# Products of key features and values moved beside the next key features in an attention and feed-forward kernel

## The reference

```python
q_prime = relu(einsum('bhnd,fd->bhnf', q, Wqf))
k_prime = relu(einsum('bhnd,fd->bhnf', k, Wkf)) * mask
kv = einsum('bhnf,bhne->bhfe', k_prime, v)
qkv = einsum('bhmf,bhfe->bhme', q_prime, kv)
qk_sum = einsum('bhmf,bhf->bhm', q_prime, k_prime.sum(2))
x = x + (qkv / (qk_sum + 1e-8)) @ Wo.T + bo
# feed-forward, on layernorm(x); rows rounded to 127 steps, weights to -1, 0, 1
activated = up * square(relu(gate))
activated = activated * rsqrt(mean(square(activated)) + 1e-6) * g
x = x + bit_linear(activated, w_down)
```

## Time and profile before

| | |
|---|---|
| median of 3 runs | 430.47 us (430.22 to 432.01) |
| profiled execution | 431.65 us, span 429.6 us |
| PE busy | 411.4 us (96%) |
| VectorE busy | 342.3 us (80%) |
| ScalarE busy | 286.5 us (67%) |
| GpSimd busy | 145.8 us (34%) |
| chain that ended last | PE 52%, DVE 21%, issue 7%, ACT 7%, POOL 6%, DMA 6% |
| DMA | 42.42 MB, mean 99 GB/s |

### The profile page before, as it was taken

How to read it: one execution, slowest core, us unless ns; L and a number is a source line. 1 busy time by engine, 2 the same in 40 slices (tenths; PEclk the granted TensorE clock), 3 DMA queues, 4 the chain that set the end, 5 groups by cost and what they waited for, 6 DMA issues and landing times.

```text
span 429.6 us, 11266 instructions
## 1 busy us (share of the span) xinstructions
PE 411.4 (96%) x4804; PEld 284.4 (66%) x4835; DVE 342.3 (80%) x505; ACT 286.5 (67%) x406; POOL 145.8 (34%) x290
## 2 busy tenths in 40 slices
PE   8989999999999999999989999999999999999995
PEld 4879899988878945844754575575567566464443
DVE  4644659658679959899986897999998798998982
ACT  5655989892155287778449747765873878939960
POOL 0000000003054722483371545547325523344660
PEclk9989999999999999999999999999999999999999
DMA  7992474632050300113323033031213021413065
GB/s 235 418 403 74 169 278 159 287 120 82 24 198 5 108 19 2 32 31 87 73 38 63 0 88 76 11 75 50 51 41 70 14 50 27 84 62 75 1 146 124
DMA packets 51170, 42.42 MB, mean 99 GB/s; under 512 B 43056, under 2 KB 44080, under 8 KB 49200
## 3 DMA queue, kind: packets, MB, share of 16 engines
q1 hardware_dynamic: 51120, 41.70, 32.9%
HBM read 27.01 MB, written 4.19 MB: 73 GB/s over the span
## 4 chain that ended last, share of the span: by engine, by line
PE 52%; DVE 21%; issue 7%; ACT 7%; POOL 6%; DMA 6%; SPq 0%; DVEq 0%; ACTq 0%
PE ps L538 11%; PE ps L407 11%; PE ps L358 6%; PE ps L360 5%; PE ps L359 5%; PE ps L555 4%; DVE zb L974 3%; PE ps L429 2%; PE ps L514 2%; DMA xqT<-xqb 2%; PE ps L448 2%; DVE rows_of L922 2%; DVE tk L985 2%; DVE qol L933 1%; DVE rows_of L917 1%
## 5 line engine op out<-in xcount | busy, mean ns | idle before, releaser
L538 PE MATMUL ps<-tg,xqT 128*128 128x512 bf16 x243 | 58.1, 380 | 4.6 <-DMA xqT<-xqb 2.9
L538 PE MATMUL ps<-tu,xqT 128*128 128x512 bf16 x245 | 59.1, 379 | 1.3 <-issue 0.6
L555 PE MATMUL ps<-td,yqT 128*128 128x512 bf16 x202 | 45.9, 379 | 1.1 <-DMA yqT<-yqb 0.7
L538 PEld LDWEIGHTS ps<-tg,xqT 128*128 128x128 bf16 x256 | 23.5, 98 | 33.1 <-DMA xqT<-xqb 4.0
L538 PEld LDWEIGHTS ps<-tu,xqT 128*128 128x128 bf16 x256 | 24.2, 98 | 31.2 <-issue 3.0
L721 ACT ACTIVATE rb<-zb 128x1024 f32<-128x1024 f32 x29 | 30.6, 1055 | 20.7 <-DVE zb L974 20.5
L974 DVE TENSOR_TENSOR zb<-ps,rb 128x1024 f32<-128x1024 f32 x29 | 35.3, 1218 | 8.2 <-ACT rb L717 8.0
L358 PE MATMUL ps<-aph,wqh 128*128 128x256 f32 x128 | 37.2, 290 | 0.0
L360 PE MATMUL ps<-aph,wkl 128*128 128x256 f32 x124 | 35.4, 286 | 1.8 <-issue 1.8
L985 DVE TENSOR_REDUCE tk<-zb 128x1 f32<-128x1024 f32 x30 | 36.2, 1207 | 1.0 <-POOL zb L1189 0.7
L358 PE MATMUL ps<-aph,wkh 128*128 128x256 f32 x124 | 36.2, 292 | 0.6 <-issue 0.6
(11 more groups left out here) (153 smaller groups left out, 1037.1 us busy)
## 6 DMA issues: line engine op xcount, KB each, us to landing
xs<-in_wg_dram SPq DMA_DIRECT2D x4, 1024.0 KB, 13.9
xs<-in_wu_dram SPq DMA_DIRECT2D x4, 1024.0 KB, 6.6
xs<-in_wd_dram SPq DMA_DIRECT2D x4, 1024.0 KB, 7.9
xs<-in_x_dram SPq DMA_DIRECT2D x8, 512.0 KB, 4.9
out_dram<-xs SPq DMA_DIRECT2D x15, 256.0 KB, 2.0
craw<-in_ctx_dram SPq DMA_DIRECT2D x7, 512.0 KB, 5.8
xs<-in_wk_dram SPq DMA_DIRECT2D x4, 256.0 KB, 5.0
xs<-in_wv_dram SPq DMA_DIRECT2D x4, 256.0 KB, 6.6
```

Source lines behind the costliest of these rows:

```text
L538: k = pe.matmul(ps[:, b0 + n, :], xqT[:, i % 3, kc, :], tern[w][:, o:o + 512], start=kc == 0, stop=kc == KC - 1)
L555: k = pe.matmul(ps[:, D_BANK[i], :], yqT(i)[:, j, :], tern[2][:, 512 * j:512 * j + 512], start=j == 0, stop=j == 15)
```

## The change

`KV_BANK` becomes 6 for every batch, so that `key_values` writes banks 6 and 7, those of `keys`. On PE the order in the key stage becomes `keys(b)`, `values(b)`, `key_values(b-1)`, `key_features(b)`. `key_values(b-1)` waits for `key_rows` 1 and 3 of batch b, and `keys(b+1)` for both copies of `key_values(b-1)`; `key_values(6)` waits for `xT_lo(1)`. `total(0)` and `total(2)` stand directly before `values`, `total(1)` between `values(3, 1)` and `key_values(2)`, which now waits for `w_mean(1)`. `U_BANK` names the banks of `up`, with the values that they had; the signals of the ternary steps are listed in the new order. From `transpose(0)` on PE's order is the same; some of its waits are other ones. The lists of ScalarE, VectorE, GpSimd and SyncE are reordered all through, most calls by one to three places. `x1_normed(0)` also waits for `key_values(7)`.

```diff
-KV_BANK = (0, 0, 0, 0, 0, 0, 0, 6)
+KV_BANK = (6, 6, 6, 6, 6, 6, 6, 6)
+U_BANK = (2, 2, 2, 2, 2, 2, 2, 2, 2, 2, 2, 2, 2, 2, 2, 2, 2, 2, 2, 2, 2, 2, 2, 2, 2, 2, 2, 6, 2, 6, 2, 6)
...
-            keys(1); values(1, 0, range(12), v_rows.at(0, 0)); key_values(0); values(1, 1, range(12))
-            key_features(1, (0, kvc_rows.at(0, 0)), (1, kvc_rows.at(0, 1))); keys(2); total(0); key_values(1)
-            values(2, 0, range(12), w_mean.at(0)); values(2, 1, range(12))
-            key_features(2, (0, kvc_rows.at(1, 0)), (1, kvc_rows.at(1, 1))); keys(3); key_values(2); values(3, 0, range(12))
-            values(3, 1, range(12)); total(1); key_features(3); keys(4, w_mean.at(1)); key_values(3)
...
+            keys(1); values(1, 0, range(12), v_rows.at(0, 0)); values(1, 1, range(12), v_rows.at(0, 1))
+            key_values(0, kT_rows.at(1, 1), kT_rows.at(1, 3)); key_features(1)
+            keys(2, kvc_rows.at(0, 0), kvc_rows.at(0, 1)); total(0); values(2, 0, range(12), w_mean.at(0))
+            values(2, 1, range(12)); key_values(1, kT_rows.at(2, 1), kT_rows.at(2, 3)); key_features(2)
+            keys(3, kvc_rows.at(1, 0), kvc_rows.at(1, 1)); values(3, 0, range(12), v_rows.at(2, 0))
+            values(3, 1, range(12), v_rows.at(2, 1)); total(1); key_values(2, w_mean.at(1)); key_features(3)
+            keys(4, kvc_rows.at(2, 0), kvc_rows.at(2, 1)); values(4, 0, range(12)); values(4, 1, range(12))
...
+            values(7, 0, range(4, 12)); key_values(6, xT_lo.at(1)); values(7, 1, range(6)); queries(0, 0, kvc_rows.at(6, 0))
...
@@ scalar, key stage @@
-            scaled_weights(0, 0); key_values_copy(1, 0); key_values_copy(1, 1)
-            for n in range(1, 4):
+            for n in range(3):
                 scaled_weights(0, n)
-            context_hi(4, 0); magnitudes(1, 0); key_rows(3, 0); magnitudes(1, 1); key_rows(3, 1); key_rows(3, 2)
-            magnitudes(1, 2); key_values_copy(2, 0); key_values_copy(2, 1); key_rows(3, 3); magnitudes(1, 3)
+            key_values_copy(1, 0); scaled_weights(0, 3); key_values_copy(1, 1); magnitudes(1, 0); context_hi(4, 0)
+            magnitudes(1, 1); key_rows(3, 0); key_rows(3, 1); magnitudes(1, 2); key_rows(3, 2); key_rows(3, 3)
+            magnitudes(1, 3); context_hi(5, 0); scaled_weights(1, 0); key_values_copy(2, 0); key_values_copy(2, 1)
...
@@ vector, around x1_rounded(4) @@
-            attended_lo(2, 0); largest(5); attended_lo(2, 1); result(1); y_scale(2); transposed_lo(6); scaled_y(4)
-            scaled_y(5); rounded_y(4); rounded_y(5); gated(7); transposed_lo(7); weighted(6); residual(4); x1_stats(4)
-            x1_moments(4); largest(6); residual(5); x1_normed(4); x1_largest(4); x1_stats(5); x1_scale(4); x1_moments(5)
-            largest(7); x1_rounded(4)
+            quotient(2, 1); attended_lo(2, 0); y_scale(2); result(1); attended_lo(2, 1); scaled_y(4); scaled_y(5)
+            rounded_y(4); rounded_y(5); transposed_lo(6); transposed_lo(7); gated(7); residual(4); x1_stats(4)
+            x1_moments(4); weighted(6); residual(5); x1_stats(5); x1_moments(5); x1_normed(4); x1_largest(4); largest(6)
+            x1_scale(4); largest(7); x1_rounded(4)
...
@@ gpsimd, first tile @@
-            x1_var(0); x1_rstd(0); x_bias(4); x_bias(5); x1_step(0); step_cubed(0); x1_weight(0); x1_weight_squared(0)
+            x1_var(0); x1_rstd(0); x1_step(0); step_cubed(0); x1_weight(0); x1_weight_squared(0); x1_var(1); x1_rstd(1)
+            x_bias(4); x_bias(5); x1_step(1); step_cubed(1); x1_weight(1); x1_weight_squared(1)
```

More of the change, by code:

```diff
@@ new lines, in tensor @@
+            keys(5, kvc_rows.at(3, 0), kvc_rows.at(3, 1)); total(2); values(5, 0, range(12)); values(5, 1, range(12))
+            key_values(4, kT_rows.at(5, 1), kT_rows.at(5, 3)); key_features(5, (2, w_mean.at(2)))
+            keys(6, kvc_rows.at(4, 0), kvc_rows.at(4, 1)); values(6, 0, range(12), v_rows.at(5, 0))
+            values(6, 1, range(12), v_rows.at(5, 1)); key_values(5, kT_rows.at(6, 1), kT_rows.at(6, 3)); key_features(6)
+            transpose(0, kvc_rows.at(5, 0)); values(7, 0, range(4), v_rows.at(6, 0)); transpose(1, kvc_rows.at(5, 1))
@@ L758, in scalar @@
+            magnitudes(2, 2); magnitudes(2, 3)
+            for n in range(4):
+                key_rows(5, n)
+            scaled_weights(2, 1); scaled_weights(2, 0); scaled_weights(2, 2); key_values_copy(4, 0); key_values_copy(4, 1)
+            context_hi(7, 0); scaled_weights(2, 3)
             for n in range(4):
@@ new lines, in vector @@
+            x_stats(14); x_stats(15); x_moments(14); x_moments(15); gated(0); inverse_error(1, 0); inverse(1, 0)
+            quotient(1, 0); inverse_error(1, 1); inverse(1, 1); quotient(1, 1); attended_lo(1, 0); attended_lo(1, 1)
+            gated(1); weighted(0); residual(2); x1_stats(2); x1_moments(2); gated(2); transposed_lo(4); transposed_lo(5)
+            weighted(1); x1_normed(2); largest(0); x1_largest(2); largest(1); x1_scale(2); weighted(2); x1_rounded(2)
+            y_scale(0); largest(2); scaled_y(1); rounded_y(0); gated(3); residual(3); x1_stats(3); x1_moments(3)
@@ new lines, in vector @@
+            transposed_lo(8); scaled_y(8); rounded_y(8); result(3); transposed_lo(9); residual(6); x1_stats(6)
+            x1_moments(6); weighted(10); gated(11); x1_normed(6); x1_largest(6); weighted(11); x1_scale(6); largest(10)
+            x1_rounded(6); largest(11); residual(7); y_scale(5); result(4); scaled_y(10); scaled_y(11); rounded_y(10)
+            rounded_y(11); x1_stats(7); x1_moments(7); x_normed(11); x1_normed(7); gated(12); x1_largest(7); x1_scale(7)
+            inverse_error(4, 0); x1_rounded(7); inverse(4, 0); quotient(4, 0); gated(13); inverse_error(4, 1); inverse(4, 1)
@@ new lines, in vector @@
+            inverse_error(5, 0); x1_rounded(9); inverse(5, 0); quotient(5, 0); weighted(16); gated(17); inverse_error(5, 1)
+            inverse(5, 1); quotient(5, 1); attended_lo(5, 0); weighted(17); largest(16); largest(17); attended_lo(5, 1)
+            gated(18); y_scale(8); result(7); scaled_y(16); scaled_y(17); transposed_lo(12); residual(10); x1_stats(10)
+            transposed_lo(13); x1_moments(10); weighted(18); x1_normed(10); x1_largest(10); residual(11); x1_scale(10)
+            gated(19); x1_rounded(10); x1_stats(11); x1_moments(11); largest(18); x1_normed(11); x1_largest(11); result(8)
@@ L1101, in gpsimd @@
+            for n in range(12, 15):
+                result(n)
+            result(15, 0); result(15, 1)
         def gpsimd(pool):
```

366 lines of the change are left out of this document (175 added, 191 removed).

## The result

| | before | after |
|---|---|---|
| median | 430.35 us (429.59 to 432.01, 4 runs) | 455.0 us (451.57 to 456.24, 4 runs) |
| ratio | 1 | 1.055 (1.051 to 1.060) |
| profiled execution, its span | 431.65, 429.6 us | 456.24, 454.2 us |
| start of `gate(0, 0)` in it | 151.43 us | 171.01 us |
| end of `key_features(6)` in it | 110.62 us | 128.32 us |

The forecast was 430.7 us, 428.5 to 433.2. The kernel became 5.5% slower. Of the 24.6 us of span, 17.7 arise before the end of `key_features(6)`, 1.9 from there to `gate(0, 0)`, and 5.0 in the feed-forward stage.

What follows compares the result with a forecast made beforehand. PE was taken as full in the key stage, with VectorE nearly full too in feed-forward. Terms +1.4 (key stage), -1.3, +0.9 and -0.75 sum to +0.25 us; forecast median 430.7 us, range 428.5 to 433.2.

Steps and rivals of the forecast that it cites:

- one new border: Key stage, key_values directly ahead of key_features: the new change of tile shape costs PE 0 to 0.20 us a batch, taken 0.10.
- Saving of neighbours: Key stage, key_values moved next to key_features in six batches: 0.10 us saved each, -0.6 us, between -1.2 and 0.
- (a): Key stage, total(0) directly before values(2, 0, w_mean): PE waits for the total and mean, +0.3 us, bounds 0 and 0.8.
- (b): Key stage, keys(3) waits for batch 1's second ScalarE copy, behind scaled_weights(0, 3): +0.5 us, bounds 0 and 1.0.
- (c): Key stage, total(1) directly before key_values(2): VectorE's value_rows(3, 1) before the mean, and late magnitudes; +1.2 us, bounds 0.8 and 2.0.
- `kT_last` and the first `xqT`, -1.3: Ahead of feed-forward: PE's waits for a key row in key_features(7) (-0.5) and first xqT (-0.8) go; bounds -1.3 and 0.
- `gate(4, 0)`, +0.9: Feed-forward, PE's 1.73 us wait for xqT(4) grows by 0.9 us through one more VectorE operation ahead; bounds 0 and 2.1.
- Feed-forward, -0.75: Waits before down(8), gate(14, 0) and in the tail shrink: face value 1.5 us, half taken, bounds -1.5 and 0.
- all other moves: 0, with 1 us either way: Remaining moves in the reordered lists were put at 0, with 1 us either way in the range.
- Case 3: Feed-forward: GpSimd's weighted(7) starts first and blocks VectorE's weighted(6), xqT(4) 2.1 us later; 431.9, with lower clock 433.1; chance 0.22.
- list of signs: PE's timeline after: expected pauses and waits; wrong if no total(1) pause, another keys block delayed, lower clock, or unnamed feed-forward waits.

Runs made afterwards that it cites:

- the thinned products: Changed kernel with key_values of batches 0 to 6 issuing only 16 of its 64 products, the others left out; 430.8 us in one run.
- the reordered lists alone: Before's lists up to the first attend, the changed kernel's behind it: 434.4 us (1.011); second kernel, also largest(3), gated(4) ahead of x1_normed(3) on VectorE: 434.1 us.
- twelve between: Changed kernel with twelve products of values put between key_values and key_features in batches 1, 2, 4, 5 and 6; 442.15 us, ratio 1.026.

## Why the prediction was wrong

The step that failed is "one new border comes, from 128x32 tiles to 32x64 tiles, which no row shows. Bounds: 0 (no cost) to 0.20". I bounded the new neighbourhood by what the engine's drain costs, and never asked whether 512 instructions of 5 to 6 ns can be delivered. The row that prices this was in the text, "PE ps L360 <- issue: 1.8, 1, 1.8". I used it for its clock and didn't ask what it was: the end of the one block in before that a burst fills almost whole. Counted from the first instruction of PE, 120 of the 128 products of `key_features(0)` and the first 8 of `keys(1)` stand in one block. By that row the change costs 6 x 1.8 = 10.8 us plus 1.2 for each fall of the clock, about 15 with three or four of them; the bound above should have been there. Measured: 13.4 and 4.5.

The other steps, one by one:
- Saving of neighbours, 0.10 a batch: `key_features` starts 1.26 us after `key_values`, whose issue alone is 1.25, so the border costs nothing that the profile shows. `keys(4)` to `keys(5)` are 16.0 us, less the pause of 1.98 = 14.0, against 14.27 for the like batch of before. 0.24 a batch, a little over my bound of 0.20. By the Trainium skill (TensorEngine Tiling (Array Packing), Key Properties) the change of mode drains the array; here no such cost appears.
- (a) `total(0)`, +0.3: a wait of 0.25. Right.
- (b) the second copy, +0.5: hidden behind the pause. Where the pause is gone, with the thinned products, PE does wait for it, 1.3 us before `keys(3)`. The mechanism was right, and its size depends on how early PE comes. There PE also waits 0.7 us before `keys(4)`, for the copies of batch 2, which I had put at nothing.
- (c) `total(1)`, +1.2: `key_values(2)` starts 1.10 us after the total's start instead of 0.21, so +0.9. The ordering on VectorE was right (0.8), the late magnitudes were not, since PE came 8 us later.
- `kT_last` and the first `xqT`, -1.3: both waits are gone. In their place PE waits 1.04 us for `xn` before `transpose(2)`, which no step names: 0.4 of 1.4 us of waits were won, and the clock of 0.80 behind the last pause took more than that back. One profile doesn't settle this term: in the two kernels of "the reordered lists alone", which have the same lists here, `key_features(7)` to `gate(0, 0)` took 17.2 us (with a wait of 1.1 for `xn`) and 16.0 (with none), for 17.1 in before.
- `gate(4, 0)`, +0.9: the wait is 1.61, 0.1 less than before. Counted from `gate(0, 0)` the load of `xqT(4)` was issued 3.1 us later (71.1 behind it for 68.0), more than I forecast. It took 2.5 us instead of 4.2, as the block of 241.29 to 242.21 was over when its data moved, and PE itself came 1.5 later, so the wait didn't grow. That is luck: 3.1 later, less 1.7 and 1.5.
- Feed-forward, -0.75: the wait before `gate(14, 0)` went, those at `down(8)` and in the tail grew, though GpSimd's `weighted(31)` fell from 3.22 to 2.36 us as I had expected. The row of "all other moves: 0, with 1 us either way" hid 2.7 us at `up(2, 1)`, `attend(3)` and around.
- Case 3 (VectorE blocked behind GpSimd) did occur at the place it names. In after GpSimd's `weighted(7)` starts 0.2 us ahead of VectorE's `weighted(6)`:

```profile
233.26 2.40 POOL L1204 TENSOR_TENSOR zb<-zb,g_b 128x1024 f32<-128x1024 f32 x1 [7.25 <-ACT rb L726]
233.46 3.28 DVE L990 TENSOR_TENSOR zb<-zb,g_b 128x1024 f32<-128x1024 f32 x1
```

  `weighted(6)` takes 3.28 us where it took 1.22 in before, 2.1 more, as the case says, and with the forecast's 0.9 these are the 3.1 us by which the load is issued later. The 3.8 us wait of PE did not come of it, for the reasons of the step above. The row of 3.28 stands in the kernel of the reordered lists alone too (at 212.1). The case's other half, a lower clock, came in the key stage, behind pauses that no case named.

My own list of signs named "a granted clock below 1.00 after 30 us" and a `keys` block delayed in another batch. Both came true: the clock fell near 40, 60, 94 and 129 us, and `keys(2)`, `keys(3)` and `keys(5)` took 1.4 to 1.5 us longer.

## What to carry to other kernels

Count instructions, not only microseconds: where a run of short instructions on one engine holds more than one block of the instruction queue, price it by the pauses of "issue" that the profile already has. Look there at whether the packets of the instruction queue land 1.4 us ahead of a resume, and whether a group of equal products is split at a place that moves by the batch's instruction count. Slow products between two bursts are cover, and a few small instructions in an idle stretch can shift a bad boundary away. Where the boundaries lie is then part of the kernel: each later edit of PE's list moves them again.

## What the runs showed of the hardware

- PE's instructions arrive in 16 KB blocks of 256. At the long pauses of after and before, 2.8 to 4.9 us pass from the crossing of one boundary to the first instruction behind the next, and 5.7 at worst: 0.4 to 2.4 us (3.3 at worst) until the fetch begins, 0.9 to 1.4 of transfer, 1.4 to 1.5 more until PE issues. A burst of 256 instructions lasts 1.25 to 1.53 us. The Trainium skill (Runtime: NRT & Kernel Launch, Instruction fetch mechanics) gives the block of 256 instructions and calls the cost of crossing one mostly hidden. The block size agrees; for PE at 5 to 6 ns an instruction the runs differ, with 12 to 15 us of pauses in a kernel.
- It also speaks of a PE memory of 2048 instructions and, beside it, of only two lines. The runs fit two: no pause in these kernels is spared by blocks fetched further ahead. But a fetch isn't tied to what PE itself issues. Where products are slow it begins up to 5.1 us before PE issues the first instruction of the block ahead (388.42 for 393.52 in before), so something reads ahead of PE; how far is open.
- What delays a fetch goes with the load on the DMA engines. At the blocks that PE had to wait for, in all these kernels, the fetch began 1.1 us after the boundary or sooner where the engines had moved nothing since, and mostly 1.6 to 4.5 us after it where they were full (1.86 at share 1.03 in before, 18.56 to 20.42). There are exceptions both ways (1.0 us with full engines in after, near 91 us; 2.0 with little traffic in before, near 100), and no run changes the load alone, so the cause is argued, not shown.
- Behind many pauses of 1.5 to 3.9 us the granted clock is at the 1.2 GHz level for about 3 us (39.99 to 43.19 in after, a product every 0.21 us for 0.12), but not behind each: `keys(4)` ran at full clock behind 1.44 us, `keys(2)` not behind 2.18, and with the reordered lists alone the clock did not fall behind 2.33 us near 22 us. In the experiment with twelve between it was 1.00 behind 0.60 and 0.79 from 52 to 60 us behind 1.75. What decides is open.
- A transposing load during which an instruction block is fetched lands 0.9 to 1.8 us later if packets of the load come behind the block. Two of 4 bytes are enough: in before the data of the load of 267.14 are over at 269.24, two such packets run at 270.17 to 270.21, behind the block of 269.23 to 270.19, and the load lands at 271.24, after 4.1 us for 2.45. In seven loads of `yqT` a block started inside but no packet ended behind it; they took 4.26 to 4.66 for 4.25. That block and packets share one of the 16 engines is read from counts (34 of 512); the records don't name the engine.
